# Fourteen operations a tile instead of nineteen in the choice of experts, and twelve of 64 shared units moved behind the mixer

## The reference: what is computed

```
x = layernorm(x + mamba(x));  x = layernorm(x + moe(x))
mamba: z, xBC, dt = split(x @ in_proj);  xBC = silu(conv4(xBC));  state scan over time with decay exp(A*dt)
       y = C.state + D*x_part;  g = y*silu(z);  return (g * rsqrt(mean(g^2)+eps) * norm_w) @ out_proj
moe:   gates = softmax(x @ router_w)  over 14 experts;  the best 2 are taken, their gates made to sum to 1
       routed = sum over the 2 chosen of gate * (silu(h @ W1) @ W2),  h = rmsnorm(x) * rms_w
       shared = the same (silu(h @ W1) @ W2) with 2 experts that every token goes through; result routed + shared
```

## Time and profile before

| | us |
|---|---|
| three timed runs | 773.78, 775.38, 776.64; median 775.38 |
| the profiled execution's own time | 774.18 |
| its span | 772.4 (14802 instructions) |
| busy in the span | PE 653.9, PEld 556.7, DVE 609.0, ACT 444.3, POOL 499.9 |
| mean granted TensorE clock | 0.923 of full speed |

### The profile page before, as it was taken

The page is one execution under the profiler, slowest core; times in us unless marked ns, Lnnn a source line. Parts: engine busy times, 40 slices in busy tenths (PEclk is TensorE's granted clock), DMA queues, the critical chain, the costliest instruction groups (busy, mean ns, idle before and its releaser), DMA issues.

```text
span 772.4 us, 14802 instructions
## 1 busy us (share of the span) xinstructions
PE 653.9 (85%) x4299; PEld 556.7 (72%) x4299; DVE 609.0 (79%) x1838; ACT 444.3 (58%) x1225; POOL 499.9 (65%) x545
## 2 busy tenths in 40 slices
PE   5987898999999999999999998875789878876730
PEld 4865676788888888888887887765688867766730
DVE  4899999999999999999999887428226423678875
ACT  4885686878767877876886654411113211336545
POOL 1144453887887797887887875665656665655561
PEclk9899998999999999999999999988789897888875
DMA  8541110221211222121121136123222232645436
GB/s 304 193 137 41 45 42 28 63 59 57 65 50 61 66 59 60 52 63 59 55 66 53 32 109 226 55 71 89 78 76 79 80 87 83 186 133 150 141 93 218
DMA packets 62639, 70.76 MB, mean 92 GB/s; under 512 B 10335, under 2 KB 45285, under 8 KB 62304
## 3 DMA queue, kind: packets, MB, share of 16 engines
q1 hardware_dynamic: 52656, 52.79, 23.1%
q0 software_dynamic: 8608, 16.87, 6.4%
q10 hardware_dynamic: 1296, 0.16, 0.1%
HBM read 48.55 MB, written 23.01 MB: 93 GB/s over the span
## 4 chain that ended last, share of the span: by engine, by line
PE 46%; DVE 16%; issue 12%; another core or an unknown queue 5%; ACT 4%; DMA 2%; SPq 1%; DVEq 0%; POOL 0%; ACTq 0%; POOLq 0%
PE bank L793 6%; PE bank L802 5%; PE bank L728 5%; PE bank L860 5%; DVE xbcT_area L1120 4%; PE bank L748 4%; PE bank L776 3%; DVE decay_area L1128 3%; PE bank L847 2%; PE bank L809 2%; PE bank L857 2%; PE bank L761 2%; PE bank L864 2%; PE bank L768 2%
## 5 line engine op out<-in xcount | busy, mean ns | idle before, releaser
L602 POOL DMA_INDIRECT returned<-xT,slots_in x141 | 141.9, 1007 | 100.2 <-DVE xT L1422 57.7
L661 POOL DMA_INDIRECT dispatched<-rows,row_u x128 | 147.7, 1154 | 31.7 <-issue 31.6
L1120 DVE SCALAR_TENSOR_TENSOR xbcT_area<-raw,conv_w,xbcT_area 128x512 f32<-128x512 f32 x162 | 127.8, 790 | 2.5 <-ACT xbcT_area L975 2.4
L728 PE MATMUL bank<-xT 128*128 128x128 f32 x564 | 90.2, 319 | 33.7 <-issue 14.6
L728 PEld LDWEIGHTS bank<-xT 128*128 128x128 f32 x564 | 82.7, 229 | 39.1 <-issue 22.1
L920 ACT ACTIVATE raw<-bank 128x512 f32<-128x512 f32 (+1 forms) x71 | 39.8, 588 | 111.7 <-remote 68.9
L1422 DVE COPY xT<-bank 128x512 f32<-128x512 f32 (+1 forms) x36 | 24.4, 677 | 95.0 <-remote 75.7
L748 PE MATMUL bank<-xbcT_area,raw 128*128 x564 | 81.8, 300 | 11.9 <-issue 11.3
L748 PEld LDWEIGHTS bank<-xbcT_area,raw 128*128 128x128 f32 x564 | 77.2, 215 | 14.3 <-issue 14.2
L1128 DVE TENSOR_TENSOR_SCAN decay_area<-decay_area,ident_heads 128x512 f32<-128x512 f32 x64 | 85.6, 1338 | 0.0
L946 ACT ACTIVATE zs<-bank 128x256 f32<-128x256 f32 x64 | 24.4, 381 | 101.9 <-PE bank L761 101.5
(11 more groups left out here) (232 smaller groups left out, 1531.8 us busy)
## 6 DMA issues: line engine op xcount, KB each, us to landing
decay_area<-decay_rows SPq DMA_DIRECT2D x64, 256.0 KB
slots_in<-dispatched SPq DMA_DIRECT2D x141, 64.5 KB
hid<-returned SPq DMA_DIRECT2D x18, 256.0 KB
xT<-xT_dram SPq DMA_DIRECT2D x8, 512.0 KB, 8.3
x<-x_dram SPq DMA_DIRECT2D x8, 512.0 KB, 7.9
out_dram<-x SPq DMA_DIRECT2D x16, 256.0 KB
xT<-returned SPq DMA_DIRECT2D x14, 256.0 KB
returned<-xT,slots_in POOLq DMA_INDIRECT x141
```

Source lines behind the costliest of these rows:

```text
L602: e.indirect_dma_start(returned, bass.IndirectOffsetOnAxis(ap=slots_in[sb_][:, n, D:ROW].bitcast(U32), axis=0), slots_out[b][:, n * P:(n + ...
L661: e.indirect_dma_start(dispatched, bass.IndirectOffsetOnAxis(ap=row_u[t % 2][:, m:m + 1], axis=0), rows[t % 3][:, k, c4, :], None).then_in ...
L728: mm = e.matmul(bank[:, off:off + P], w1_now[b][:, k * P:(k + 1) * P], slotsT[gr % len(slotsT)][:, n % 4 * P:(n % 4 + 1) * P], start=True, ...
L1120: e.scalar_tensor_tensor(o, r[:, n:n + W], conv_w[:, k, TAPS - 1 - n:TAPS - n], o, ALU.mult, ALU.add).then_inc(S["conv"])
```

## The change

1. `choose` loses the cast of the indices and does both comparisons in one operation over 128x112, with the uint32 indices read as they are. `rows_to_take` makes `row_of` and the next tile's starting row in one operation over 128x70, both products in one over 128x112, and takes a maximum (one entry of 14 is not zero) straight into uint32. `choose` and `rows_to_take` together have 14 operations a tile, not 19.
2. Units of the shared experts are placed by a table. Up to step 64 the steps with i % 4 == 3 have none (12 units fewer by then); steps 68, 70, 72, 74 and 76, which have no routed group, have two; the rest of the steps have one, and so have the first groups behind the loop: units 61, 62 and 63 beside groups 11, 12 and 13, the halves 64 to 67 (L793 alone) beside groups 14 to 17.
3. The carving of `xT` is reordered and three waits take the place of one, at `hidden` >= 28, at 32, 36 and 40 for the three output buffers, and at 48 for `gexp`.

```diff
+    units = {i: 1 for i in range(LAG, LAST + NC) if i > NC or i % 4 != 3}
+    for i in range(NC + 3, min(ROUTED_AT[-1], NC + 13)):
+        if i not in ROUTED_AT:
+            units[i] = 2
+    unit_ends, units_so_far = {}, 0
+    for i in sorted(units):
+        units_so_far = min(units_so_far + units[i], NC + 4)
+        unit_ends[i] = units_so_far
     def shared_units(i):
-        return [i - LAG] if 0 <= i - LAG < NC + 4 else []
+        return range(unit_ends.get(i - 1, unit_ends.get(i - 2, 0)), unit_ends[i]) if i in unit_ends else []
+    def beside_group(gr):
+        return LAST + gr - GROUPS_IN_LOOP
...
             for gr in range(GROUPS_IN_LOOP, GROUPS):
+                shared_experts(beside_group(gr))
                 routed_group(gr)
...
-                e.tensor_copy(top_f[:], top_i[:, :, 0:TOP_K]).then_inc(S["top"])
-                for k in range(TOP_K):
-                    e.tensor_tensor(hot[:, k], expert_no.unsqueeze(1).to_broadcast([P, 4, NR]), top_f[:, :, k:k + 1].to_broadcast([P, 4, NR]), ALU.is_equal).then_inc(S["hot"])
+                chosen_no = top_i[:, :, 0:TOP_K].rearrange("p c k -> p k c").unsqueeze(3).to_broadcast([P, TOP_K, 4, NR])
+                e.tensor_tensor(hot[:], expert_no.unsqueeze(1).unsqueeze(1).to_broadcast([P, TOP_K, 4, NR]), chosen_no, ALU.is_equal).then_inc(S["hot"])
...
-                e.tensor_tensor(row_of[:], bank[:, 0:4 * NR].rearrange("p (c r) -> p c r", r=NR), now[:].unsqueeze(1).to_broadcast([P, 4, NR]), ALU.add).then_inc(S["rows_taken"])
-                e.tensor_tensor(then[:], bank[:, 4 * NR:n5], now[:], ALU.add).then_inc(S["rows_taken"])
-                for k in range(TOP_K):
-                    e.tensor_tensor(row_hot[:, k], hot[:, k], row_of[:], ALU.mult).then_inc(S["rows_taken"])
-                e.tensor_reduce(row_f[:], row_hot[:].rearrange("p k c r -> p (k c) r"), AX.X, ALU.add).then_inc(S["rows_taken"])
-                e.tensor_copy(row_u[t % 2][:], row_f[:]).then_inc(S["rows_taken"])
+                e.tensor_tensor(of[:], bank[:, 0:n5].rearrange("p (c r) -> p c r", r=NR), now.unsqueeze(1).to_broadcast([P, 5, NR]), ALU.add).then_inc(S["rows_taken"])
+                e.tensor_tensor(row_hot[:], hot[:], of[:, 0:4, :].unsqueeze(1).to_broadcast([P, TOP_K, 4, NR]), ALU.mult).then_inc(S["rows_taken"])
+                e.tensor_reduce(row_u[t % 2][:], row_hot[:].rearrange("p k c r -> p (k c) r"), AX.X, ALU.max).then_inc(S["rows_taken"])
...
-                    on.wait_ge("hidden", AREA_UNITS)
+                    on.wait_ge("hidden", SLOTST_UNITS)
```

More of the change, by code:

```diff
@@ L217, in mamba_moe @@
     for gr in range(GROUPS_IN_LOOP, GROUPS):
+        act_uses += [("hidden", u) for u in shared_units(beside_group(gr)) if u < NC]
         if gr + 2 < GROUPS:
@@ L783, in tensor_program @@
                     tr.then_inc(S["gT"])
[L784 to L802, removed]
+                shared_experts(i)
                 c = i - 5
@@ L934, in by_token, with hidden_of_shared @@
                     normalise(s - 2, "x2")
+            def hidden_of_shared(i):
+                for u in shared_units(i):
+                    if u < NC:
+                        on.wait_ge("hidden", u + 1)
+                        was = u - NHID
+                        if was >= 0:
+                            on.wait_ge("down", 4 * (was // 4) + 4)
+                        on.wait_ge("dt_step", 3 * DT_CHAIN)
+                        e.activation(hid[u % NHID][:], act_ring.bank("hidden", u)[:], ACT.Silu).then_inc(S["hidden_silu"])
             dt_exp(0)
@@ L983, in scalar_program @@
                     e.activation(gT[c % 2][:].rearrange("p k i -> p (k i)"), act_ring.bank("gT", c)[:, 0:DI], ACT.Copy).then_inc(S["gT_copied"])
[L984 to L992, removed]
+                hidden_of_shared(i)
                 t = due(i, 11)
@@ L1295, in tables @@
             def tables():
-                now = next_row[NT % 2]
+                now = row_of[(NT - 1) % 2][:, 4, :]
                 by_expert = expert_no.unsqueeze(1)
@@ L1314, in tables @@
                 on.wait_ge("gated", NC)
-                step(e.tensor_copy(fill_row[:], now[:]))
-                last = step(e.tensor_copy(totals[:, SEGS - 2], now[:]))
+                step(e.tensor_copy(fill_row[:], now))
+                last = step(e.tensor_copy(totals[:, SEGS - 2], now))
                 after(last)
@@ L1420, in routed_group @@
                     on.wait_ge(f"returned{b}", 64 * (gr // len(slots_out)))
+                on.wait_ge("hidden", OUT_UNITS[b])
                 cols = slice(0, len(slot_tiles(gr)) * P)
@@ L1512, in by_token, with shared_add @@
                             ln_shift(u, 1, 3 * NT + 2 * n + 2)
+            def shared_add(i):
+                for u in shared_units(i):
+                    if u >= 4 and u % 4 == 3:
+                        t = (u - 4) // 4
+                        on.wait_ge("down", 4 * t + 4)
+                        on.wait_ge("x1", 4 * t + 4)
+                        e.tensor_tensor(x[:, 4 * t:4 * t + 4, :], down_bank[:].rearrange("p (c d) -> p c d", c=4), x[:, 4 * t:4 * t + 4, :], ALU.add).then_inc(S["shared_added"])
             later = steps_of(0)
@@ L1562, in vector_program @@
                     ln_shift(t, 2, 3 * t + 3)
-                for u in shared_units(i):
-                    if u >= 4 and u % 4 == 3:
-                        t = (u - 4) // 4
-                        on.wait_ge("down", 4 * t + 4)
-                        on.wait_ge("x1", 4 * t + 4)
-                        e.tensor_tensor(x[:, 4 * t:4 * t + 4, :], down_bank[:].rearrange("p (c d) -> p c d", c=4), x[:, 4 * t:4 * t + 4, :], ALU.add).then_inc(S["shared_added"])
+                shared_add(i)
                 if i == NC + 2:
```

73 lines of the change are left out of this document (46 added, 27 removed).

## The result

The changed kernel is slower by 0.2 to 0.6 per cent. In the first comparison it took 780.68 us (median of 779.19, 779.98, 781.39 and 782.12) where the kernel before took 775.34: ratio 1.0059, interval 1.0040 to 1.0078. A second comparison gave 778.19 us against 776.51: 1.0018, 1.0002 to 1.0035. The forecast was 769.7.

The account below looks back on a forecast made before the run. PE and DVE both full in the mixer, a ring of POOL's scatters and DVE's copy behind it; -13.3 + 1.35 + 6.3 = -5.65 us, from 775.38 to 769.7 us; own range 764 to 775, over all cases 761.5 to 783.5.

Parts of the forecast that it names:

- Mixer: Steps 14 to 63: eleven convolution tiles 1.0 us shorter each, plus two other tiles; together -13.3 us, bounds 6.8 to 21.
- DVE becomes the bound and a tile should take 26.3: Mixer tiles: PE falls to 25.55 us, DVE to 26.3, so DVE sets the pace and a tile is 1.0 us less.
- My lower bound of 0.4 us a tile: Mixer tiles: least gain, 0.4 us, from small savings and a DVE that is at 27.2.
- whole 1.75 us: Step 63: DVE has no convolution there, so PE's full saving of one unit, 1.75 us, counts.
- Entry: Steps 62 and 64: fewer rounds of DVE's chains delay the early table that SyncE's first slot loads need: +1.35 us.
- PE already waits 2.38 us for these slots: Entry: PE already waits for SyncE's first slot loads, so nothing covers the early table's delay: +1.35 us.
- Behind the mixer: Routed stage: twelve added units +9.5, shorter choose and rows_to_take -1.2, PE's clock -2: 6.3 us longer.
- The 2 us credited for the clock: Behind the mixer: with more PE work in between, one or two clock falls should go: -2 us (0 to -5).
- Full price: Behind the mixer, units cost their full length: +19.8 for 6.3, so 783.2 us; sign: group 17's copy not earlier; chance 0.24.
- Hidden: Behind the mixer, units cost next to nothing because POOL's scatters pace it: -11.4 us, so 764.0 us; chance 0.14.
- DVE gives little: Mixer: DVE partly waits for memory shared with POOL; tile falls 0.4 us, loop gains 6.75, 776.3 us; chance 0.12.
- The clock once a tile: Mixer: PE's 0.75 us wait a tile lets its clock fall; loop gains 4.75, 778.3 us; chance 0.05.

Follow-up runs that it names:

- e1: Changed kernel's fourteen operations alone, units placed as in the kernel before: 772.99 us, ratio 0.9973.
- e2: Kernel before with only the moved units, shared_experts and areas, keeping its nineteen operations: 782.85 us, ratio 1.0085.
- e9: Changed kernel unchanged, run again as the second comparison: 778.19 us, ratio 1.0018.
- e12: Kernel before unchanged, run for its trace on the second comparison's chip: 775.25 us in its one time.
- e13: Changed kernel with SyncE's load of w1_routed issued ahead of the slots: 769.05 us, ratio 0.9942.
- e17: Kernel before with SyncE's load of w1_routed issued ahead of the slots: 775.85 us, ratio 0.9985.
- e10: Changed kernel leaving out most of PE's work for the twelve units, waits kept: 773.33 us, ratio 0.9938.
- e5: Changed kernel leaving out most of PE's work for the five second units of steps 68 to 76, on the 729 us chip: ratio 0.9935.
- e8: Changed kernel with six units moved, not twelve, on the 729 us chip: ratio 0.9967.

## Why the prediction was wrong

The signs of its three terms were right, and their sum was not: -5.65 forecast, +5.2 in the two traces (last copies). Of the 10.9 us between them 5.65 lie in the mixer, 2.95 at the entry and 2.3 behind it.

**Mixer, -13.3 forecast, -7.65 measured.** The term that failed, and the largest miss, is "DVE becomes the bound and a tile should take 26.3". DVE's own work did fall to 26.0 us a tile, but it no longer works 99 per cent of the time: once PE has a gap, each waits for the other at the matrix products' hand-over (1 us of PE on `mix` a tile), and the tile is 26.79. My lower bound of 0.4 us a tile was near the number, but by luck: it was made from small savings and "a DVE that is at 27.2", and DVE's saving was full. The "whole 1.75 us" of step 63 did not come either: the lead was 8.10 us at the scan of chunk 59 (418.07 for 426.17) and 7.65 at the last one. Between the scans of chunks 14 and 19 the lead grew by 1.6 us, for 0.6 forecast. But e1 and e2 show at least as much against that one trace of before, and e9 against e12 shows 0.3, so it belongs to that trace; by e9 and e12 the mixer gave 6.58 in all.

**Entry, +1.35 forecast, +4.3 measured** (7.65 less the 3.39 of L747), the step that could be undone by one edit. I placed `row_early` rightly, behind the four L1586; 2.0 us of lead are lost there, for 1.35. Another 1.5 are lost between `row_early` and the landing of group 1's slots (14.67 us after it, 13.17 before), and 0.75 behind the wait, where the clock is down. What I did not do is follow SyncE's queue behind `row_early`: "PE already waits 2.38 us for these slots" was taken to be a wait for `row_early`, and it was one for 1792 KB in front of group 1. I had also priced that stage with a full lead of the mixer, though the wait said that PE was already early. By my signs PE's wait should have been near 3.7 us; it was 5.88. e13 and e17 show the cause: one load, moved, is worth 1 us to the kernel before and 6 to 9 to the changed one.

**Behind the mixer, +6.3 forecast.** By e9 and e10 the work costs 4.9 to 6.2 us (for 16.3 of its 21.0 us), against 9.5 forecast for the units alone: step 68 cost 2.0 for 1.75; in step 70 PE does wait for `shared_added` (1.48 us at 484.88), but steps 70 to 76 together cost 0.6 for 1.75; the other 3.6 came beside groups 4 to 17 (3.4) and behind them, for 6.0 forecast. In the first two traces the stage lost more, 8.4 us from L747 to group 17 (a lead of 3.39 turned into -5.00), for 6.3 forecast. The 2 us credited for the clock did come as PE time. Of the two slow sets of sixteen in the earlier trace rows one became fast:

```profile
513.41 1.95 PE L747 MATMUL bank<-xT 128*128 128x128 f32 x16
538.48 3.62 PE L747 MATMUL bank<-xT 128*128 128x128 f32 x16
```

From 506 to 536 us the granted clock is 1.00 for 0.86 before, and 0.76 from 540 to 560 us in both. In e9 and e12 the sets take 1.95 for 3.07 and 2.44 for 3.75. No run shows whether any of it reached the end, and why the stage still lost 2.1 us more than forecast stays open. The account is -7.65 + 4.3 + 8.4 + 0.2 behind group 17 = +5.2.

**The rivals.** Full price: by my own sign, group 17 not earlier than 626.0, it would be called true, and its 783.2 us is nearer to the 780.68 measured than the forecast. As a mechanism it has fallen, since taking 16.3 us of the work out gave back 6.2 (e9 and e10); the sign was a bad one, for the lead can also be lost in front of that stage, and was. Hidden: fallen too (e10). DVE gives little: its 0.4 us a tile was nearer to the 0.53 than my 1.0, but for another reason, since DVE's saving was full. The clock once a tile: fallen, 1.00 with waits of up to 1.6 us. What the Trainium skill says in "TensorE: Matmul & The Clock Gate", section "HAM oscillation", that waits between batches can put the clock down each time, did show where PE waits 5.88 us at the entry (eight L782 in 1.91 us, for 1.06 in the earlier trace rows) and not in the mixer.

**Left open.** e10 leads by 3.4 us over e12 at group 0 and by 1.7 at the end; two traces of the kernel before differ by 1.7 us there (750.59 and 752.32), so this may be nothing. Why PE and DVE meet so that two savings give 0.5 to 0.6 us a tile and not 1.0 was read from the waits and from e1 and e2; no run moved the hand-over itself. Why the changed kernel was 0.6 per cent slower once and 0.2 the other time was not found out.

## What to carry to other kernels

When work is taken out in front of a hand-over, follow each queue past it, to the last transfer that the next stage needs, and ask what now lands last: a load that was just in time is the next bound, and moving its issue up can be worth more than the work removed. Two engines that were both full gave here, when both were relieved (by 0.68 and 1.75 us a tile), less than the smaller relief; measure each alone (0.1 and 0.1 a tile here, 0.25 and 0.16 over the longer stretch) and both (0.5 and 0.63) before adding them up. Work moved to where engines look idle costs where its wait or its place in the queue comes before what the next stage needs.

## What the runs showed that I had not expected

The stretches in which PE's matmuls start about 1 us apart and DVE stands (up to 8.5 us) while POOL issues eight indirect DMAs in a row were there on some chips and not on others. On the four chips where the kernel before takes 774.6 to 777.7 us they are there in the traces; on the fifth, in e5 to e8, they are not; POOL's eight DMAs take the same 0.97 us each, 0.3 us apart, and the kernel before takes 729.24. I have no mechanism. A price read inside such a stretch holds for such a chip only: the late units cost 3.6 of the 6.2 us on a chip of 775 and nothing that shows on the fifth, where the five second units cost 4.5 us and not 2.6. Two halves of one study should run on one chip, with the changed kernel beside them.
